# The last column group of a graph-network kernel: one chunk of four turned by VectorE in three of its five pairs, and most of its row sums made by ScalarE

## The reference

```
layer 0: e = x with a small product per row;  h = adj @ (adj.T @ e);  layernorm(h) * gamma + beta + its input
layer 1: adj @ x
layer 2: Chebyshev terms: adj @ x three times in a row, each with a 64 x 64 weight
layer 3: degree = row sums of (adj + I);  relu(D^-1/2 (adj + I) D^-1/2 (x W + b))
```

## Time and profile before

| | us |
|---|---|
| median of 3 runs | 1448.79 (1447.44 to 1451.46) |
| the profiled execution | 1448.4 |
| its span, first to last instruction | 1446.2 |
| TensorE matmul busy | 1419.2 (98%) |
| VectorE busy | 491.8 (34%) |
| ScalarE busy | 399.3 (28%) |
| GpSimd busy | 84.4 (6%) |
| DMA, mean over the span | 362 GB/s |

### The profile page before, as it was taken

How to read it: one execution, slowest core, us unless ns; L and a number is a source line. 1 busy time by engine, 2 the same in 40 slices (tenths; PEclk the granted TensorE clock), 3 DMA queues, 4 the chain that set the end, 5 groups by cost and what they waited for, 6 DMA issues and landing times.

```text
span 1446.2 us, 18473 instructions
## 1 busy us (share of the span) xinstructions
PE 1419.2 (98%) x7601; PEld 600.5 (42%) x7601; DVE 491.8 (34%) x1082; ACT 399.3 (28%) x885; POOL 84.4 (6%) x67
## 2 busy tenths in 40 slices
PE   6999999999999999999999999999999999999998
PEld 3555555555555563333333333333333333333332
DVE  6694544544546533331132211011311121101044
ACT  2378778677776551000000000000000000000000
POOL 2210000000000038000000000000000000000000
PEclk9999999999999999999999999999999999999999
DMA  9999999999999998999996797899797948996998
GB/s 322 382 422 409 419 414 413 419 410 411 412 402 371 391 420 341 420 421 420 421 409 215 320 363 295 320 352 323 302 336 263 312 179 357 392 377 227 356 419 316
DMA packets 97607, 523.26 MB, mean 362 GB/s; under 512 B 18764, under 2 KB 18804, under 8 KB 54644
## 3 DMA queue, kind: packets, MB, share of 16 engines
q1 hardware_dynamic: 90436, 520.40, 91.4%
q10 hardware_dynamic: 7088, 1.67, 0.5%
HBM read 415.88 MB, written 106.17 MB: 361 GB/s over the span
## 4 chain that ended last, share of the span: by engine, by line
PE 78%; DMA 16%; ACT 3%; DVE 2%; POOL 1%; issue 1%; SPq 0%; ACTq 0%; POOLq 0%; DVEq 0%
PE turned L640 33%; PE acc L640 29%; DMA raw<-in_adj_dram 13%; PE t_acc L651 8%; PE turned L673 5%; ACT staged L882 3%; DMA over_wide<-adj_t 2%; PE turned L828 1%; DMA w_in<-in_L_gnn_W_i_dram 0%; PE t_rows L812 0%; PE turned L834 0%; DVE staged L1174 0%; PE acc L703 0%; ACT over_last L882 0%; PE t_acc L802 0%
## 5 line engine op out<-in xcount | busy, mean ns | idle before, releaser
L1134 DVE STREAM_TRANSPOSE staged<-raw 32x256 f32<-32x256 f32 x448 | 195.1, 435 | 5.8
L651 PE MATMUL t_acc<-raw,E 128*64 128x384 f32 (+1 forms) x1120 | 185.3, 478 | 5.1 <-DMA raw<-in_adj_dram 5.0
L882 ACT ACTIVATE staged<-turned 128x512 f32<-128x512 f32 x303 | 152.7, 636 | 104.1 <-PE turned L673 103.7
L926 ACT ACTIVATE t_t<-raw 128x768 uint8<-128x768 f32 (+1 forms) x216 | 177.2, 901 | 0.0
L640 PE MATMUL acc<-staged,t_cur 128*64 128x512 f32 x720 | 161.1, 596 | 0.0
L673 PE MATMUL turned<-ident,raw 128*128 128x128 f32 x1376 | 159.5, 274 | 0.0
L673 PEld LDWEIGHTS turned<-ident,raw 128*128 128x128 f32 x1376 | 149.8, 140 | 21.7 <-issue 21.7
L640 PE MATMUL turned<-over_last,C 128*64 128x512 f32 x672 | 152.1, 592 | 0.0
L651 PEld LDWEIGHTS t_acc<-raw,E 128*64 128x64 f32 x1120 | 78.4, 138 | 109.3 <-issue 85.7
L1277 POOL TENSOR_TENSOR rstd<-rstd,minus_half 128x8 f32<-128x8 f32 (+1 forms) x30 | 44.2, 1475 | 1265.9 <-DVE rstd L1036 1265.9
L640 PE MATMUL turned<-over_last,R 128*64 128x512 f32 x512 | 116.5, 593 | 0.0
(11 more groups left out here) (139 smaller groups left out, 1061.9 us busy)
## 6 DMA issues: line engine op xcount, KB each, us to landing
over_last<-adj_t SPq DMA_DIRECT2D x181, 1024.0 KB, 9.1
staged<-adj_t SPq DMA_DIRECT2D x91, 1024.0 KB, 9.4
raw<-in_adj_dram SPq DMA_DIRECT2D x60, 1536.0 KB, 19.5
adj_t<-staged SPq DMA_DIRECT2D x30, 3072.0 KB, 18.0
over_wide<-adj_t SPq DMA_DIRECT2D x23, 1024.0 KB, 7.7
raw<-in_adj_dram SPq DMA_DIRECT2D x10, 1024.0 KB, 15.0
adj_t<-over_last SPq DMA_DIRECT2D x8, 1024.0 KB, 14.9
adj_t<-C SPq DMA_DIRECT2D x2, 1024.0 KB, 21.7
```

Of the source, the lines that this page charges most:

```text
L651: last = nc.tensor.matmul(t_acc[h * D:(h + 1) * D, 0:columns], E[:, m * SUB + a, :], raw_of(g, m)[:, a, h * columns:(h + 1) * columns], st ...
L882: nc.scalar.activation(turned_into(g, u)[:, i * B:(i + 1) * B], turned[n % TURN_BANKS][:, :], ACT.Copy) \
L926: nc.scalar.activation(passed[n % 2][:, 0:chunks(g) * P], raw_of(g, m)[:, a, :], ACT.Copy, accum_out=deg_part[:, m * SUB + a, g:g + 1]).th ...
L1134: last = nc.vector.transpose(dst[b * SQ:(b + 1) * SQ, :, :, q * SQ:(q + 1) * SQ], src[q * SQ:(q + 1) * SQ, :, :, c * P + b * SQ:c * P + (b ...
```

## The change

In the last group `by_vector` now holds for pairs 0, 1 and 3: VectorE turns their chunk 3, TensorE and ScalarE leave out two of eight banks in each. VectorE's chunk of pair 0 comes in group 5, behind `add_h` of its pair 3, that of pair 1 at u = 0, that of pair 3 at u = 4, ahead of that u's `end_of_layer`. It waits for the turning and for both row sums of the pair before, over whose raw blocks it writes. The sums of blocks 0, 2, 4 and 6 of the last group go from VectorE to ScalarE; those of blocks 8 and 9 stay with VectorE and move from u = 0 to u = 1, behind `add_h` of pair 0.

```diff
-VECTOR_FROM, VECTOR_LAST = 2, 0
+VECTOR_FROM, VECTOR_LAST = 2, (0, 1, 3)
...
-            return m < VECTOR_LAST if g == NG - 1 else pair_no(g, m) >= VECTOR_FROM
+            return m in VECTOR_LAST if g == NG - 1 else pair_no(g, m) >= VECTOR_FROM
...
-        ACT_SUMS = [x for x in PAIR_SUMS if 0 < x[0] < NG - 1 or x[0] == NG - 1 and x[1] % 2 == 1 and x[1] < NB - 2]
+        ACT_SUMS = [x for x in PAIR_SUMS if 0 < x[0] < NG - 1 or x[0] == NG - 1 and x[1] < NB - 2]
...
                     if g < NG - 1:
                         wait_stage_free(dve, g, m)
-                    elif m >= 1:
-                        wait_turned(dve, g, m - 1)
                     else:
-                        wait_turned(dve, g - 1, ROWS - 1)
+                        before = (g, m - 1) if m >= 1 else (g - 1, ROWS - 1)
+                        wait_turned(dve, *before)
+                        for b in range(2):
+                            wait_summed(dve, before[0], 2 * before[1] + b)
...
                 for u in range(UNITS):
                     if u % 2 == 1:
                         add_h(g, u // 2)
-                    if u == 0:
+                    elif u + 2 < UNITS:
+                        turn_chunk(g, u // 2 + 1)
+                    if u == 1:
                         for x in sums_of(g, 0):
                             sum_rows(*x)
                     end_of_layer(u)
```

## The result

The changed kernel takes 1456.23 us (median of 6 runs, 1453.82 to 1456.68) against 1449.79 us for the kernel before in the same comparison: ratio 1.0042, 95% interval 1.0029 to 1.0055, so 4 to 8 us slower. The forecast was 1453.5 us, 4.7 us slower. The profiled execution took 1456.14 us with a span of 1453.9, for 1446.2 before: +7.7 us in the trace.

A forecast was written before the change was run, and what follows sets the result against it. TensorE, 98% busy, was taken as bound, with VectorE's norms' round nearly as long in the last group. Round delay +5.9 less 1.2 given back is +4.7, on 1448.79 giving 1453.5 us; range 1452.0 to 1455.0, wide 1450.0 to 1457.2.

The forecast's parts named there:

- Pair 0's saving is worth 0: TensorE before 508.2 us: pair 0's 0.89 us saved counts for nothing, as TensorE then waits 1.00 us for DMA.
- Pair 1: -0.8, pair 3: -0.89: TensorE, last group: fewer transposes save 0.8 us in pair 1 and 0.89 in pair 3, together 1.7 us by 533 us.
- ScalarE's sums, pairs 0 and 1, the moved sums: hidden: ScalarE's 2.5 us more per pair in group 5, and VectorE's early chunks and moved sums, fit in idle time.
- The chunk of pair 3 takes 7.17 us and stays in the round: VectorE at u = 4: chunk runs 530.4 to 537.6 us; variances of h follow at 537.6, 545.4 and 553.2.
- L725 of pair 2, both waits ending together at 540.3: TensorE's `rows_of_h` of pair 2, behind pair 4's late banks and `add_h`, comes at 540.3 for 537.30: 3.0 us late.
- L725 of pair 3 at 548.4, of pair 4 at 556.2: TensorE's `rows_of_h`, paced by the norms' round: +5.7 us for pair 3, +5.9 for pair 4, starting the second part.
- SP's late stores cost nothing: SP's queue: stores of units 7 to 9 go at 537.6, no cost taken; at most the last lands 3 us later.
- 1.2 us are given back: Second part: TensorE, late, no longer meets three waits for loads; 0.7 to 1.3 us returned, 1.2 taken.
- a granted clock under 1.00 between 534 and 560 us: TensorE's clock: listed among the observations in the profile after that would show the forecast wrong.
- rival (c): TensorE's clock also falls in the new stage, 3.6 us more if lasting into the second part: up to 1457.1; chance 0.15.
- both stands that it named: TensorE standing idle 4.2 us (about 534.1 to 538.3) and 3.6 us (544.8 to 548.4).
- rival (a): VectorE's chunk at u = 4 takes at most 2.8 us, TensorE keeps its saving: 1447.1, or 1448.0 us; chance 0.08.

The follow-up runs named there:

- e2: The changed kernel with only pairs 0 and 1 given to VectorE; 1450.13 us for 1450.19 of the kernel before, ratio 1.0004.
- e4: The changed kernel with only pairs 1 and 3 given to VectorE; 1453.32 us for 1450.19 of the kernel before, ratio 1.0029.
- e5: The changed kernel with pair 3's chunk at u = 3, ahead of the centring, not u = 4; 1451.81 us for 1450.57 of the kernel before, ratio 1.0008.
- e11: The changed kernel measured again, unaltered, on the chip of e12; ratio 1.0033 to the kernel before.
- e1: The changed kernel with no chunks given to VectorE, only the sums moved; 1449.46 us for 1450.19 of the kernel before, ratio 0.9996.
- e6: The changed kernel with four unused matmuls in TensorE's stand before pair 4's last four banks; ratio 1.0039 to the kernel before.
- e8: The changed kernel with pairs 1 and 2 given to VectorE, all last-group sums to ScalarE; 1449.05 us for 1450.57 of the kernel before, ratio 0.9990.
- e3: The changed kernel with only pair 3 given to VectorE; 1453.78 us for 1450.19 of the kernel before, ratio 1.0036.
- e10: The kernel before, with seven second-part loads no longer waiting for the last two stores to land; 1448.75 us for 1450.69, ratio 0.9986.
- e12: The changed kernel with two unused matmuls in TensorE's wait ahead of the last raw block's t product; ratio 1.0026 to the kernel before.

## Why the prediction was right

Step by step. To compare instants, the forecast's are moved by the 1.5 us by which A is later in this profile and, from the early fall on, by its 1.6 us: 3.1 us in all.

- *Pair 0's saving is worth 0.* Right, and more than that: the wait became 1.93 us for 1.00, 0.9 us longer, as e2 has it too.
- *Pair 1: -0.8, pair 3: -0.89.* Right: A to first L725 is 12.1 for 12.87 in e2, e4, e5 and e11, and from there to the next L725 it is 7.24 us in the changed kernel for 8.12 before.
- *ScalarE's sums, pairs 0 and 1, the moved sums: hidden.* Right (e1, e2).
- *The chunk of pair 3 takes 7.17 us and stays in the round.* Right: 7.17 measured, variances behind it 7.80 and 7.78 us apart, forecast 7.80. With both shifts, the forecast's 537.6, 545.4 and 553.2 become 540.7, 548.5 and 556.3; measured 540.61, 548.41 and 556.19.
- *L725 of pair 2, both waits ending together at 540.3.* The term that was off: with the shifts 543.4, measured 544.76, as the sixteen transposes behind the stand ran at half clock (3.57 us). It had no effect on the end (e6). For the same reason TensorE stood 1.94 us before L725 of pair 3 and not the 3.6 of the forecast.
- *L725 of pair 3 at 548.4, of pair 4 at 556.2.* 551.5 and 559.3 with the shifts, 551.34 and 559.35 measured. For pair 4 VectorE was no longer the last: its `add_h` ended at 559.11, and TensorE, slowed by the late fall, came to L725 0.2 us behind that.
- *SP's late stores cost nothing.* The result is right, the reason given for it isn't: I had transfers in flight across the gap. DMA ran nearly dry (share 0.20 from 537.2 to 541.2), the stores went at 540.66 and later. It was free because the first load, at 559.52, waited for TensorE's first tile by then (its product ran from 557.53 to 559.41) and not for a store.
- *1.2 us are given back.* 1.3 measured (895.9 to 894.6), and no wait for loads is left behind B.

The sum: 5.9 - 1.2 = 4.7 us forecast; e4, the changed kernel without the idle wait's side effect, measured 4.2 us (2.6 to 5.7) and 6.0 - 1.1 = 4.9 by its trace. The changed kernel itself lies at 4.2 to 8.0 us in one comparison and 2.9 to 6.5 in the other. What the sum left out is the clock's fall near 510 us, 1.6 us in the profile. The forecast had a narrow range of 1452.0 to 1455.0 with a chance of 0.55, and the median of 1456.23 lies 1.2 us above it; the wide range of 1450.0 to 1457.2 holds it. The kernel before was itself 1.0 us slower in this comparison than the 1448.79 that the forecast started from, and the early fall is about the rest. So the mechanism is right, and the size is right to within a term that the sum didn't have.

One of the prediction's own signs of being wrong did show: a granted clock under 1.00 between 534 and 560 us. It was rival (c), to which it gave 0.15, and it came in both stands that it named. It had no weight there, since the first is covered and the second costs 0.2 us: the product behind it took 4.48 us for 3.65, not twice as long. I had put the clock among the rivals but looked for its cost at the wrong stand; the one that counts is a wait of 1.9 us, ahead of the round. A small slip: rival (a) with pair 3's part alone would be 1447.9 us, not 1448.0.

The Trainium skill's rule that transposes don't count as activity (TensorE: Matmul & The Clock Gate, Part 4) doesn't hold here after the change either: from 541.35 to 544.76 us TensorE ran nothing but transposes, and at 544.69 us the clock was back at 1.00. The return isn't always so quick: in e11 the clock fell at 540.47 us, the same sixteen transposes began at 541.32, and it stayed at 0.50 until 547.30.

## What to carry to other kernels

What it costs to move work from the engine that bounds the kernel to one that is 34% busy depends on where the work lands in that engine's order. Look for a round that passes through the receiving engine, compare its length (7.8 us here) with what the bound engine needs in the same time (8.1), and put the work where the receiving engine has idle time to hold it. Ahead of the round it cost nothing (e2, e8), in a gap of 3.3 us inside the round it cost about 1 us (e5), behind that gap 5 us (e3). Then ask what paces the next stage: time saved ahead of a wait for DMA only lengthened the wait (e2), and the stores that the next stage's loads waited for were the cheaper thing to change (e10).

## What the runs showed that was not expected

The granted clock fell to 0.50 behind waits of TensorE much shorter than the 4.1 us that it had stood through at the end of the kernel before: behind 1.93 and 2.27 us in the changed kernel and e6, and not behind 1.92 and 2.48 us in e2 and e11. So the length of one wait alone does not tell. With the stands of 4.18 us it fell in each of the five profiles that have one (changed, e3, e4, e11, e12), and stayed low for 3.4 or for 6.8 us.

A late fall came with TensorE's wait before L725 of pair 3 in five profiles: changed, e4, e5, e6 and e12, with waits of 1.94, 2.01, 2.86, 3.40 and 1.79 us. It is not wholly covered. In these five L725 of pair 4 starts 0.23 to 0.31 us behind the end of VectorE's `add_h`, in all others 0.05 or 0.06: it costs about 0.2 us. In the profiles the early fall is the only one that costs more.
